# The second term of the experts' down product in bfloat16, and the slots' rows loaded by another engine

## The reference

```
probs = softmax(layernorm(x) @ gate_w.T)            # 8 experts
top-2 of probs, normalized                          # w: token x expert
out = swiglu(xn, sWg, sWu, sWd)                     # shared expert
for e in range(8):
    out += w[:, e] * ((silu(xn @ Wg[e]) * (xn @ Wu[e])) @ Wd[e])
```

## Time and profile before

| what | value |
|---|---|
| time, median of 3 runs | 2139.71 us (2135.65 to 2140.8) |
| the profiled execution's own time | 2137.79 us |
| its span, first to last instruction | 2136.1 us |
| granted TensorE clock, mean | 0.983 |
| PE busy | 1957.2 us (92%) |
| DVE busy | 1246.5 us (58%) |
| ACT busy | 1065.7 us (50%) |
| POOL busy | 820.6 us (38%) |

### The profile page before, as it was taken

The page is one execution under the profiler, slowest core; times in us unless marked ns, Lnnn a source line. Parts: engine busy times, 40 slices in busy tenths (PEclk is TensorE's granted clock), DMA queues, the critical chain, the costliest instruction groups (busy, mean ns, idle before and its releaser), DMA issues. The chain is left out here.

```text
span 2136.1 us, 48445 instructions
## 1 busy us (share of the span) xinstructions
PE 1957.2 (92%) x14755; PEld 1296.5 (61%) x14824; DVE 1246.5 (58%) x3875; ACT 1065.7 (50%) x2310; POOL 820.6 (38%) x1206
## 2 busy tenths in 40 slices
PE   2689999999999999999988999997999999999997
PEld 1345445454454544545435788886777777777776
DVE  5666667766667666776662865553445545444553
ACT  1255555555555555555552345452555555555553
POOL 4033323333323333233332037773444444444443
PEclk9799999999999999999999999999999999999999
DMA  7234443344443434434322346654863333333332
GB/s 240 60 106 117 121 136 124 110 118 119 136 130 107 122 111 140 128 114 124 100 87 79 137 134 226 223 188 150 215 167 58 57 55 55 56 55 57 54 57 34
DMA packets 156641, 246.08 MB, mean 115 GB/s; under 512 B 29408, under 2 KB 90592, under 8 KB 156480
## 3 DMA queue, kind: packets, MB, share of 16 engines
q1 hardware_dynamic: 120960, 189.24, 28.9%
q0 software_dynamic: 32064, 53.44, 12.2%
q10 hardware_dynamic: 3456, 1.34, 0.3%
HBM read 111.89 MB, written 90.50 MB: 95 GB/s over the span
## 5 line engine op out<-in xcount | busy, mean ns | idle before, releaser
L680 DVE CUSTOM_DVE_ANT_0 ps_rows<-ps_rows,maskrow 128x128 f32<-128x128 f32 (+1 forms) x1009 | 477.1, 514 | 290.9 <-PE ps_rows L525 282.2
L623 ACT ACTIVATE probs<-ps_cols 128x512 f32<-128x512 f32 (+3 forms) x1024 | 392.0, 435 | 386.7 <-PE ps_cols L536 380.1
L525 PE MATMUL ps_rows<-ks,qs 32*128 32x512 f32 x1984 | 403.1, 480 | 73.5 <-DVE mx L680 38.6
L532 PE MATMUL ps_cols<-qs,ks 32*128 32x512 f32 (+3 forms) x2048 | 418.5, 485 | 2.5 <-ACT probs L623 2.4
L1642 POOL DMA_INDIRECT out_dram<-y_e,to x135 | 216.1, 1601 | 349.4 <-DMA out_dram<-y_e,to 221.5
L799 POOL TENSOR_TENSOR pace<-eps 1x1 f32<-1x1 f32 x256 | 58.2, 227 | 747.0 <-ACT probs L623 747.0
L525 PEld LDWEIGHTS ps_rows<-ks,qs 32*128 32x128 f32 x1984 | 153.3, 184 | 268.5 <-DVE mx L680 221.9
L536 PE MATMUL ps_cols<-mT,ones_r 32*128 32x512 f32 (+3 forms) x1024 | 284.8, 550 | 0.0
L1771 DVE TENSOR_TENSOR h_lo<-ps_h,h_hi 128x512 fp32r<-128x512 f32 x135 | 93.3, 691 | 232.6 <-ACT h_hi L1746 232.6
L1740 ACT ACTIVATE sg_e<-ps_ge 128x512 f32<-128x512 f32 x135 | 80.7, 598 | 263.1 <-PE ps_ge L1664 261.0
L554 PE MATMUL ps_o<-probs,vt 128*32 128x512 f32 (+3 forms) x2048 | 192.5, 448 | 0.8 <-POOL probs L801 0.8
(11 more groups left out here) (220 smaller groups left out, 3838.9 us busy)
## 6 DMA issues: line engine op xcount, KB each, us to landing
xs_d<-zrows SPq DMA_DIRECT2D x45, 408.0 KB, 2.9
xr<-xs_d POOLq DMA_DIRECT2D x135, 136.0 KB, 3.3
whi_d<-w_sh SPq DMA_DIRECT2D x16, 768.0 KB, 3.8
w_hi<-whi_d SPq DMA_DIRECT2D x24, 512.0 KB
xn<-in_L_attn_x_dram SPq DMA_DIRECT2D x16, 512.0 KB, 5.2
ks<-k_lin SPq DMA_DIRECT2D x64, 128.0 KB, 3.0
ks<-k_tan SPq DMA_DIRECT2D x64, 128.0 KB, 3.7
qs<-q_lin SPq DMA_DIRECT2D x64, 128.0 KB, 2.4
```

The source lines that it names most:

```text
L525: mm = nc.tensor.matmul(ps_rows[bank_of(row_no(g, it, h))][:, 0:(it + 1) * P], qs[at:at + STRIP, d.par, g, it * P:(it + 1) * P], ks[at:at ...
L532: nc.tensor.matmul(ps_cols[bank_of(col_no(n, s, e))][:, jt * P:S], ks[at:at + STRIP, b.par, gc, jt * P:(jt + 1) * P], qs[at:at + STRIP, b. ...
L623: nc.scalar.activation(probs[:, n % 2, 2 * (1 - s) + e, jt * P:S], ps_cols[bank_of(col_no(n, s, e))][:, jt * P:S], ACT.Exp).then_inc(exp_d ...
L680: nc.vector.tensor_tensor_reduce(out=bank, in0=bank, in1=maskrow[:, (TT - 1 - it) * P:S], scale=1.0, scalar=LOWEST, op0=ALU.add, op1=ALU.m ...
```

## The change

In the down product the third-listed term, h_lo·w_hi, takes bfloat16 on both sides: `h_lo` becomes a bfloat16 tile, and its moving operand is a new tile `w_db`, the bfloat16 rounding of w_hi of Wd. POOL makes it from `w_sh` in `split` (one more copy for each of the two pieces of Wd in a batch, into `w_sb`), SP stores it to a new DRAM array and loads it back with the expert's third matrix. The order of the three terms stays as it was. Gate and up products stay as they were.

The rows of the slots are loaded by POOL up to the step of slot 25, and by SP from the step of slot 26 on, behind the last of the weights' loads. For that `over_slots` has two loops where it had one on PE and POOL (5 rounds, four slots written out, 26 rounds), and PE waits on another semaphore (`x_handed`) for rows that SP loaded. POOL waits for `to_ready` ahead of a scatter.

```diff
-    GU = KT * INTER
+    GU, HANDED = KT * INTER, 27
+    w_db = sb("w_db", [P, NE, GU], BF16)
-    h_lo = sb("h_lo", [P, 2, IT, P], F32R)
+    h_lo = sb("h_lo", [P, 2, IT, P], BF16)
...
             w = [t[:, bass.ds(e, 1), m].rearrange("p o n -> p (o n)") for t in (w_hi, w_lo)]
-            for at, (part, side) in enumerate(((hi, 0), (bf, 1), (lo, 0))):
+            if m == 2:
+                w.append(w_db[:, bass.ds(e, 1)].rearrange("p o n -> p (o n)"))
+            for at, (part, side) in enumerate(((hi, 0), (bf, 1), (lo, 2 if m == 2 else 0))):
...
+            if m == 2:
+                nc.gpsimd.tensor_copy(w_sb[:, half], w_sh[:, m, half].bitcast(F32)).then_inc(w_cast, 1)
...
+            sp.wait_ge(w_cast, (b.v + 1) * 2)
+            sp.nop(nofuse=True)
+            sp.dma_start(wdb_d[ex, :, k], w_sb[:]).then_inc(w_out, 16)
...
+    def load_rows(eng, s, loaded):
+        eng.wait_ge(tx_ready, s.v + 1)
+        eng.nop(nofuse=True)
+        eng.wait_ge(to_ready, s.v + 1)
+        eng.nop(nofuse=True)
+        eng.wait_ge(share_ready, s.v + 1)
+        eng.nop(nofuse=True)
+        eng.dma_start(xr[:, s.par], rows_of(xs_v, s.plus(2))).then_inc(loaded[s.par], 16)
...
+                if m == 2:
+                    sp.dma_start(w_db[:, e], wdb_d[e].rearrange("p k n -> p (k n)")).then_inc(w_loaded, 16)
+        load_rows(sp, Batch(0, HANDED - 1), x_handed)
+        after_hand(sp, lambda s: load_rows(sp, s, x_handed))
+        for s in range(NSLOT - 4, NSLOT - 2):
+            load_rows(sp, Batch(0, s), x_handed)
...
+            if by_pool:
+                pe.wait_ge(x_loaded[s.par], (s.half() + 1) * 16)
+            else:
+                pe.wait_ge(x_handed[s.par], (s.half() - HANDED // 2) * 16)
```

More of the change, by code:

```diff
@@ L140, in build @@
     wlo_d = nc.dram_tensor("wlo_d", [NE, P, 3, KT, S], BF16, kind="Internal").ap()
+    wdb_d = nc.dram_tensor("wdb_d", [NE, P, KT, S], BF16, kind="Internal").ap()
     x1_d = nc.dram_tensor("x1_d", [NB, P, TT, D], F32, kind="Internal").ap()
@@ L163, in build @@
                                 rec_d, x1_d, xs_d, ident, ones, mv2, eps, xs_zeroed,
-                                lns, lnb, gwT, gws, gwb, lgT, Wg, Wu, Wd, whi_d, wlo_d, (sWg, sWu, sWd), shared)
+                                lns, lnb, gwT, gws, gwb, lgT, Wg, Wu, Wd, whi_d, wlo_d, wdb_d, (sWg, sWu, sWd), shared)
             pos = sbt(mid, "pos", [P, NT, 2], I32)
@@ L172, in build @@
         with ExitStack() as c:
-            expert_stage(nc, c, sbt, whi_d, wlo_d, xs_d, out, ident, slot_e)
+            expert_stage(nc, c, sbt, whi_d, wlo_d, wdb_d, xs_d, out, ident, slot_e)
 def attention_stage(nc, ctx, sbt, x_v, wqT, bq, wkT, bk, wvT, bv, woT, bo, J, lam,
                     rec_d, x1_d, xs_d, ident, ones, mv2, eps, xs_zeroed,
-                    lns, lnb, gwT, gws, gwb, lgT, Wg, Wu, Wd, whi_d, wlo_d, shared_weights, shared):
+                    lns, lnb, gwT, gws, gwb, lgT, Wg, Wu, Wd, whi_d, wlo_d, wdb_d, shared_weights, shared):
     def sb(name, shape, dt=F32):
@@ L334, in attention_stage @@
     w_sl = sb("w_sl", [P, 3, S], BF16)
+    w_sb = sb("w_sb", [P, S], BF16)
     ps_rows = [ctx.enter_context(nc.psum_tensor(f"ps_rows{r}", [P, S], F32)) for r in range(3)]
@@ L370, in attention_stage @@
     w_split = sem("wp_split")
+    w_cast = sem("wp_cast")
     w_out = sem("wp_out")
@@ L810, in split @@
                     pool.nop(nofuse=True)
-                    pool.wait_ge(w_out, b.v * 32)
+                    pool.wait_ge(w_out, b.v * 48)
                 pool.nop(nofuse=True)
@@ L975, in _ @@
         sp.wait_ge(xs_zeroed, NSLOT // ZR * 16)
-        sp.wait_ge(w_out, NB * 32)
+        sp.wait_ge(w_out, NB * 48)
 class SharedExpert:
@@ L1534, in _, with expert_stage @@
             beside()
-def expert_stage(nc, ctx, sbt, whi_d, wlo_d, xs_d, out, ident, slot_e):
+def expert_stage(nc, ctx, sbt, whi_d, wlo_d, wdb_d, xs_d, out, ident, slot_e):
     def sb(name, shape, dt=F32):
@@ L1573, in expert_stage @@
     x_loaded = [sem(f"xe_loaded{r}") for r in range(2)]
+    x_handed = [sem(f"xe_handed{r}") for r in range(2)]
     tx_ready = sem("tx_ready")
@@ L1592, in expert_stage, with over_slots, after_hand @@
     out_v = out.rearrange("b s d -> (b s) d")
-    def over_slots(eng, step):
+    def over_slots(eng, step, until=None):
+        until = until or step
         for s in range(3):
[L1597 to L1600, removed]
+            until(Batch(0, s))
+        if until is step:
+            with eng.Fori(0, (NSLOT - 7) // 4) as i:
+                for s in range(3, 7):
+                    step(Batch(i, s, 4))
+        else:
+            with eng.Fori(0, (HANDED - 3) // 4 - 1) as i:
+                for s in range(3, 7):
+                    until(Batch(i, s, 4))
+            for s in range(HANDED - 4, HANDED):
+                until(Batch(0, s))
+            after_hand(eng, step)
         for s in range(NSLOT - 4, NSLOT + 2):
             step(Batch(0, s))
+    def after_hand(eng, step):
+        with eng.Fori(0, (NSLOT - 4 - HANDED) // 4) as i:
+            for s in range(HANDED, HANDED + 4):
+                step(Batch(i, s, 4))
     def exists(s):
@@ L1622, in _, with step_loading @@
             pool.dma_start(xr[:, r], xs_v[r]).then_inc(x_loaded[r], 16)
+        def step_loading(s):
+            if s.at_most(HANDED - 2):
+                load_rows(pool, s, x_loaded)
+            step(s)
         def step(s):
[L1625 to L1633, removed]
             if exists(s.plus(-2)):
@@ L1636, in step @@
                 pool.wait_ge(y_taken, d.v + 1)
+                pool.nop(nofuse=True)
+                pool.wait_ge(to_ready, d.v + 1)
                 pool.nop(nofuse=True)
@@ L1644, in step @@
                     .then_inc(y_stored[d.par], 16)
-        over_slots(pool, step)
+        over_slots(pool, step, step_loading)
         for r in range(2):
@@ L1666, in product, with turn_rows @@
             return mm
-        def turn_rows(s):
-            pe.wait_ge(x_loaded[s.par], (s.half() + 1) * 16)
+        def turn_rows(s, by_pool):
+            if by_pool:
+                pe.wait_ge(x_loaded[s.par], (s.half() + 1) * 16)
+            else:
+                pe.wait_ge(x_handed[s.par], (s.half() - HANDED // 2) * 16)
             if s.at_least(1):
@@ L1705, in down, with step @@
                     (hh_ready, hb_ready, hl_ready), s.v + 1).then_inc(y_ready, 1)
-        def step(s):
+        def step(s, by_pool=False):
             if exists(s):
@@ L1717, in step @@
             if s.at_most(NSLOT - 2):
-                turn_rows(s.plus(1))
+                turn_rows(s.plus(1), by_pool)
             if exists(s):
                 up(s, e)
-        turn_rows(Batch(0, 0))
-        over_slots(pe, step)
+        turn_rows(Batch(0, 0), True)
+        over_slots(pe, step, lambda s: step(s, True))
     @block.scalar
```

2 lines of the change are left out of this document (1 added, 1 removed).

## The result

The changed kernel takes 2190.51 us (median of 4 runs, 2186.05 to 2191.88), the kernel before beside it 2140.26 us (4 runs, 2135.65 to 2142.35): ratio 1.0228, 95% interval 1.0211 to 1.0245. It is slower by 50 us. Forecast were 2178 and +38; the range reached to 2193.

What follows compares the result with a forecast made beforehand. PE's array was taken as the bound, its sequencer as the bound after the change: +40 us, less 0.4 for the array, is +39.6 on 2137.8, so 2177.4; forecast 2178 against a median of 2139.7, range 2160 to 2193.

Steps and rivals of the forecast that it cites:

- PE's sequencer becomes the bound: Expert stage: the sequencer's need rises to 20.35 to 20.45 us a round against the array's 19.15, costing 40 us; chance 82%.
- 0.12 us an operation: Price of each added register operation on PE, four more a slot, 1.95 us a round of four slots.
- Rivals one and two: One: operations stay hidden, array remains the bound, 2135 to 2140 us, 8%. Two: hidden in part, 2140 to 2165, 6%.
- The sequencer's own need, "I take 18.4": PE's sequencer work before the change in a round of 19.15 us: 18.4 us, bounds 18.2 to 18.6.
- The second reading in the prediction: Sequencer's need from a 4.6 us slot without waits, four such plus the loop's branch: 18.8 us a round, an upper bound.
- The slots written out: The 11 expert-stage slots outside the loops, with no branch and fewer address computations: no cost taken there.
- The row loads, "worth nothing": Moving expert-stage row loads from POOL to SP: no gain or loss; SP's first load due at 1601 or 1608 us.
- The scatter chain: POOL, scatter to scatter 4.74 us with the row load between; can only shorten without row loads, far from the bound.
- The array's gain, 0.03 to 0.04 us a slot: Cheaper bfloat16 last block on PE: 4 to 5 us in all if the array bounds, 0.4 us with the sequencer as bound.
- The third rival: The array gains much more, a bfloat16 block 0.18 us cheaper, 24 us in all, time 2115 us; chance 4%.
- Attention and weights at nothing: POOL's extra copies, SP's extra store and longer weight loads are covered: 0 taken, attention's range -1 to +2 us.
- What the profile after would show: Expected signs: slots of 5.1 us, twelve operations at 0.12 us, PE some 95% busy, scatters waiting for DVE's y.

Runs made afterwards that it cites:

- e1: The kernel before, with the down product's last term taking its weights from up's hi part, so 16 more register operations a round, still float32r: 2185.7 us.
- e2: The changed kernel, with the down product's last term, bfloat16, taking w_lo at the middle term's addresses, so no added operations ahead of matmuls: 2142.1 us.
- e3: The changed kernel, with two of the last term's four matmuls taking w_lo at addresses already set, so 8 added operations a round ahead of matmuls: 2158.7 us.
- e7: The changed kernel without the hand-over: one loop, all rows loaded by POOL, no added wait ahead of the scatter: 2187.2 us.
- e4: The changed kernel with float32r in the last term as before; third weight copy still made, stored and loaded, SP still loads rows: 2142.7 us.
- e6: The changed kernel, with two of four down products in a round keeping the expert register that the gate had loaded, 2 register loads fewer: 2177.6 us.
- e5: The changed kernel, with three of the last term's four matmuls taking w_lo at addresses already set, so 4 added operations a round ahead of matmuls: 2148.7 us.

## Why the prediction was right, and where its size was off

*PE's sequencer becomes the bound.* Shown: e1 adds the operations and nothing else and loses 46 us, e2 leaves them out and keeps everything else and loses 3.

*0.12 us an operation.* Shown by e3 against the changed kernel (0.96 us for 8). The Trainium skill ("Advanced Engine Details and Errata", "Engine Queue Depths") gives TensorE a queue of 64; the prediction weighed that by this alone the operations would stay hidden. They do not: they come in every slot, and e1's lengthened round shows no lead that bridges them. Rivals one and two are out. (For rival two the prediction's own formula gives 18.4 + 1.6 + 0.1 = 20.1 us and 2169 at 0.1 an operation, not the 2165 that it names.)

*The sequencer's own need, "I take 18.4".* This is the term that was mis-sized. The runs give 18.66, above the 18.6 of the prediction's upper bound. The reading had found 0.6 to 0.7 us of waiting in a round of 19.15 and took away still more, "since the slots without waits may hide small ones". They don't: in the changed kernel, whose sequencer waits for nothing, the shortest instances of a round's 152 steps add up to 20.20 us and the round takes 20.66. Such small variations are its own. The same sum of shortest steps in the kernel before is 18.17 us; with the same 0.46 on top it is 18.63, so the two ways agree. The round grew by 1.50 in place of 1.3, over 31 rounds 46 us in place of 40. The second reading in the prediction, from a slot without waits (18.8), was nearer. The slots written out cost next to nothing, as taken (the four between the loops 19.8 us, where a round took 19.16 before): the rounds' 5 x 1.42 + 26 x 1.50 = 46 is the whole of the stage's +45.6.

*The row loads, "worth nothing".* Wrong by 3.0 us, POOL's DRAIN at the end, which the prediction had no term for. 46 + 3 = 49 of the 50 us. The sum itself was also set down 1 us low: 2177.4 and the 1.9 between that execution and the median are 2179.3, not 2178. So the time lies near the top of the range, 2193, and e7, without the DRAIN's 3 us, at 2187. SP's first issue did come in time, 4 us later than the 1608 forecast for a stage that here began 5 us later:
```profile
L1643 SPq DMA_DIRECT2D xr<-xs_d x107: 332/333/358, 1611.7 to 2158.8; - x107
```
The scatter chain, which "can only shorten", did not. Timeline of POOL in e4, where nothing but the row loads has left it and slots take 4.79 us:
```profile
1898.54 1.55 POOL L1681 DMA_INDIRECT out_dram<-y_e,to  x1 [3.83 <-DVE to L1840]
1903.21 1.55 POOL L1681 DMA_INDIRECT out_dram<-y_e,to  x1 [3.12 <-DVE to L1840]
1907.83 1.55 POOL L1681 DMA_INDIRECT out_dram<-y_e,to  x1 [3.07 <-DVE to L1840]
```
They are 4.67 and 4.62 us apart (4.74 in the earlier trace rows). The profile puts these three waits down to DVE's `to`, but that copy belongs to a later slot, and the scatter's own y was ready some 2 us earlier. From 1700 to 2100 us most waits of the scatters are put down to the landing of the scatter before (us, times, longest), first e4, then the changed kernel:
```profile
POOL out_dram L1681 <- DMA out_dram<-y_e,to: 251.4, 78, 3.8
```
```profile
POOL out_dram L1681 <- DMA out_dram<-y_e,to: 196.1, 56, 4.0
```
That is 78 of 84 scatters in e4, 56 of 78 in the changed kernel. So the chain from scatter to landing to scatter takes some 4.75 us without a row load in between too, just under the slot, and would still be next in the way of a faster PE; whether it has a part in e2's small gain was not tried. In the changed kernel, with 5.16 us a slot, it is not the bound: e7 has the same stage, and there 64 of 78 scatters wait for DVE's y.

*The array's gain, 0.03 to 0.04 us a slot.* The size of the block was right, the sum halved at least: 1 to 2 us in e2 where 4 to 5 were taken. It didn't matter for the forecast. The third rival, 0.18 us a slot, is out.

*Attention and weights at nothing.* Right: e4 has both and begins its expert stage as before. POOL's new copy in attention:
```profile
745.25 0.78 POOL L818 TENSOR_TENSOR w_sl<-w_st,w_sh 128x256 bf16<-128x256 f32 x1
745.98 0.39 POOL L821 CAST w_sb<-w_sh 128x256 bf16<-128x256 f32 x1
749.05 0.18 POOL L802 TENSOR_TENSOR pace<-eps 1x1 f32<-1x1 f32 x1 [2.69 <-ACT probs L626]
```
0.39 us, with 2.69 idle behind it.

*What the profile after would show.* Slots came at 5.16 us on average (5.1 forecast), with twelve operations in a row, the passed wait, the idle time put down to issue and the 98 ns. "PE busy at some 95% or less" was wrong: it reads 98.9%. So was "waiting for DVE's y" for POOL's scatters: 56 of 78 waits are put down to the landing before, two to y.

## What to carry to other kernels

Count what an engine's sequencer does between its instructions, in steps from start to start and not in busy time. An edit that makes the data cheaper but gives each matmul an address of its own can cost more than it gains: here 0.04 us a slot for 0.48. Put a new operand where its address follows from one that is already set, or leave it.
When a bound is a sequencer, look for the wait that it will run into next before counting on a saving. In e6 three quarters of it went into a wait for h that cost nothing before.

## What the hardware showed that was not expected

- POOL's DRAIN at the end of the program took 3.82 us with all rows loaded by POOL, 6.80 with the hand-over at slot 27 or 79, and 3.25 at 127. Each value came again to the nanosecond in every kernel of its kind (3822 in four, 6802 in nine). What sets it stays open; it was not tried apart from the hand-over.
- PE reads 98.9% busy in the changed kernel, 99.3 before, while its slots come 7% more slowly at a granted clock of 1.00. Its busy share can't tell an array that is full from one that is fed late.
- Two needs that are nearly equal need not give the larger of them: with the array at 19.09 and the sequencer at some 19.2 us the round took 19.32 (e5).
- Moving the row loads off POOL didn't shorten its chain of scatters: 4.7 to 4.8 us from one to the next with them (before) and without (e4), nearly all of it one scatter and its landing.
